# Expert one-hots, routing shares, block comparisons and head squares: other engines and other places in the queues

## The reference, cut to what matters

```
def L1_attn(x):                       # 16 heads of 16, blocks of 32 keys
    q, k, v = rope(x @ Wq.T), rope(x @ Wk.T), x @ Wv.T
    gate = q . mean of k over each block           # 8 blocks
    gate = -1e30 for later blocks, +1e30 for the own block
    sel = the 4 blocks with the highest gate
    p = softmax(q k^T / 4 where sel and causal)
    o = p @ v
    o = o * rsqrt(mean(o * o) + 1e-6) * o_norm_w   # for each head
    return o @ Wo.T

def L1_ffn(x):                        # F = 896, 8 experts of rank 32, top 2
    rw, sel = top_k(softmax(x @ Wg.T), 2); rw = rw / rw.sum()
    for k in range(2):
        mask = one_hot(sel[:, k])
        x1 = x @ W1.T + low_rank(A1, B1, mask)     # x3 the same way
        x2 = silu(x1) * x3
        out += (x2 @ W2.T + low_rank(A2, B2, mask)) * rw[:, k]
```

## Time and profile before

| | before |
|---|---|
| median of 3 runs | 714.51 us (713.04 to 714.55) |
| the profiled execution | 714.51 us, span 712.7 us |
| PE, DVE, ACT, POOL busy | 680.5, 491.6, 409.7, 284.7 us |
| chain that ended last | PE 77%, DVE 13%, ACT 5% |
| mean granted TensorE clock | 0.993 |

### The profile page before, as it was taken

One profiled execution on the slowest core, in us unless ns is written; L12 is line 12 of the kernel. 1 busy time (PEld: TensorE's weight loads), 2 busy tenths in 40 slices (PEclk: granted clock), 3 DMA queues, 4 the chain that ended last, 5 costly groups with the idle time before them and its releaser, 6 DMA issues.

```text
span 712.7 us, 13698 instructions
## 1 busy us (share of the span) xinstructions
PE 680.5 (95%) x4708; PEld 580.4 (81%) x4708; DVE 491.6 (69%) x1422; ACT 409.7 (57%) x1069; POOL 284.7 (40%) x289
## 2 busy tenths in 40 slices
PE   4999999999999999998999998999989999999997
PEld 3677888888889888887785655666889999999997
DVE  5898877877878787777695786767565454644544
ACT  2756158788797888888212578888753312222221
POOL 0573245556465554541004218999333320400000
PEclk9999999999999999999899999999999999999999
DMA  8902034453435354351900000200300000000000
GB/s 312 350 0 93 5 111 135 150 161 125 164 118 169 116 163 129 97 166 44 402 20 1 1 0 3 104 2 2 119 1 1 2 2 16 1 16 1 2 16 15
DMA packets 26725, 59.42 MB, mean 83 GB/s; under 512 B 3147, under 2 KB 12749, under 8 KB 26273
## 3 DMA queue, kind: packets, MB, share of 16 engines
q1 hardware_dynamic: 23584, 50.35, 20.7%
q0 software_dynamic: 3072, 8.20, 3.4%
HBM read 48.24 MB, written 10.49 MB: 82 GB/s over the span
## 4 chain that ended last, share of the span: by engine, by line
PE 77%; DVE 13%; ACT 5%; issue 3%; DMA 1%; POOL 0%; SPq 0%; DVEq 0%; ACTq 0%
PE bank L2164 11%; PE bank L1944 7%; PE bank L1878 6%; PE bank L2187 5%; PE bank L1935 5%; PE bank L2213 5%; PE bank L1964 4%; PE bank L1885 3%; PE bank L1955 3%; PE bank L2075 3%; PE bank L2006 3%; PE bank L2227 2%; PE bank L2133 2%; PE bank L2099 2%; ACT sb L1135 2%
## 5 line engine op out<-in xcount | busy, mean ns | idle before, releaser
L1031 ACT ACTIVATE sb<-bank,sb 128x256 f32<-128x256 f32 x128 | 59.6, 471 | 40.6 <-DVE sb L1497 33.1
L1497 DVE TENSOR_REDUCE sb<-bank 128x2 f32<-128x512 f32 x64 | 43.7, 683 | 47.5 <-PE bank L1944 47.1
L1944 PE MATMUL bank<-sb 128*128 128x256 f32 x256 | 66.1, 381 | 0.0
L1200 ACT ACTIVATE h_parts<-sb 128x256 fp32r<-128x256 f32 x56 | 23.4, 418 | 71.3 <-DVE sb L1733 43.4
L1724 DVE TENSOR_TENSOR sb<-sb,bank 128x256 f32<-128x256 f32 x56 | 23.5, 419 | 59.0 <-ACT sb L1164 59.0
L2164 PE MATMUL bank<-rounded,b_hi 128*128 128x256 f32 x224 | 63.6, 284 | 0.0
L2164 PE MATMUL bank<-rounded,b_lo 128*128 128x256 f32 x224 | 63.4, 283 | 0.0
L2164 PE MATMUL bank<-am_lo,b_hi 128*128 128x256 f32 x224 | 63.4, 283 | 0.0
L1164 ACT ACTIVATE sb<-bank 128x256 f32<-128x256 f32 x56 | 21.5, 383 | 63.4 <-PE bank L2164 63.3
L1038 ACT ACTIVATE sb<-sb 128x256 f32<-128x256 f32 x128 | 57.7, 504 | 0.1
L815 POOL DMA_INDIRECT expert_out<-sb x32 | 33.1, 1034 | 60.1 <-DVE sb L1439 44.2
(11 more groups left out here) (302 smaller groups left out, 1936.6 us busy)
## 6 DMA issues: line engine op xcount, KB each, us to landing
sb<-in_w_gate_up SPq DMA_DIRECT2D x32, 368.0 KB
sb<-in_w_down SPq DMA_DIRECT2D x32, 256.0 KB
sb<-in_w_pair SPq DMA_DIRECT2D x8, 704.0 KB
expert_out<-sb SPq DMA_DIRECT2D x1, 4096.0 KB, 22.5
sb<-expert_out SPq DMA_DIRECT2D x8, 512.0 KB, 7.3
sb<-in_w SPq DMA_DIRECT2D x1, 1792.0 KB, 13.8
sb<-in_b SPq DMA_DIRECT2D x1, 1792.0 KB, 7.0
sb<-in_sw_up SPq DMA_DIRECT2D x1, 1536.0 KB, 9.9
```

Of the source, the lines that this page charges most:

```text
L1031: act.activation(probs[:, u % 4, q, :], bank[3 + u % 2][:, q * S:(q + 1) * S], ACT.Exp, scale=-1.0, bias=row_min[:, u % 4, q:q + 1], accum ...
L1497: dve.tensor_reduce(row_min[:, u % 4, :], bank[3 + u % 2][:, :].rearrange("p (q n) -> p q n", q=QT), AX.X, ALU.min).then_inc(at_min, 1)
L1944: mm = pe.matmul(bank[3 + u % 2][:, q * S:(q + 1) * S], qb[i][:, h, b * S + q * P:b * S + (q + 1) * P], keys[:, h, b * S:(b + 1) * S], sta ...
```

## The change

- `expert_of` is made by DVE alone, in 16 instructions of 128x256 with the chosen expert as a per-partition scalar. The two small `one_of` and the two spreads on ACT go.
- The shares are transposed in two groups of eight, at j = 1 and j = 2, into banks 2 and 7, and DVE copies them out in its steps j = 1 and 2. The four `share_out` on ACT go. TensorE waits for the last copy at j = 3 and not at j = 5.
- All seven comparisons for the other sequences lie in DVE's loop steps: d = 1, 2, 3 at j = 0, d = 4, 5 at j = 1, d = 6, 7 at j = 2.
- The squares are one instruction at the end of s = 1, both sums and the epsilon come in s = 2, the root in s = 3 between `hidden_high(3, 0)` and `activated(1, 1)`, and the reciprocal at the end of DVE's s = 3.

```
 # POOL
-            pool.wait_ge(r1_step, 10 + 2 * NT)
+            pool.wait_ge(r1_step, 8 + 2 * NT)
 # ACT
-                if n == 3:
-                    for k in range(2):
-                        act.wait_ge(r1_step, 8 + 2 * NT + k)
-                        act.activation(expert_of[k].rearrange("p t (e r) -> p (t e) r", r=R1),
-                                       along(one_of[k].rearrange("p t e -> p (t e)"), (2, R1)), ACT.Copy).then_inc(r1_own, 1)
...
-            def share_out(n):
-                act.wait_ge(fill_mm, len(fills()) + n + 1)
-                act.activation(shareT[:, n // 2, n % 2 * CH:(n % 2 + 1) * CH], bank[SHARE_BANK[n]][:, :], ACT.Copy)\
-                    .then_inc(fill_out, 1)
...
-                if 0 < j < 5:
-                    share_out(j - 1)
...
+                if s == 3:
+                    act.wait_ge(on_step, 3)
+                    act.activation(o_sd, o_var, ACT.Sqrt).then_inc(on_act, 1)
...
-                if s in (1, 2):
-                    half = slice((s - 1) * HALF * H1, s * HALF * H1)
+                if s == 1:
                     act.wait_ge(bl_o, QUADS)
-                    act.activation(squares[:, half, :], o_tok.rearrange("p t (h d) -> p (t h) d", d=D1)[:, half, :], ACT.Square)\
-                        .then_inc(on_act, 1)
-                if s == 3:
-                    act.wait_ge(on_step, 3)
-                    act.activation(o_sd, o_var, ACT.Sqrt).then_inc(on_act, 1)
+                    act.activation(squares, o_tok.rearrange("p t (h d) -> p (t h) d", d=D1), ACT.Square).then_inc(on_act, 1)
 # DVE
             for k in range(2):
-                dve.tensor_tensor(one_of[k], along(table("iota")[:, 0:E1], (1, NT)), along(chosen1[:, :, k], (2, E1)),
-                                  ALU.is_equal).then_inc(r1_step, 1)
+                for i in range(NT):
+                    dve.tensor_scalar(expert_of[k][:, i, :].rearrange("p (e r) -> p e r", r=R1),
+                                      along(table("iota")[:, 0:E1], (2, R1)), chosen1[:, i, k:k + 1], None,
+                                      ALU.is_equal).then_inc(r1_own, 1)
...
-            for d in (1, 2, 3, 4):
-                compare(dve, rest_heads, beats_rest, rest_beats, d)
...
+            def shares_out(k, c):
+                dve.wait_ge(fill_mm, len(fills()) + 2 * k + c + 1)
+                dve.tensor_copy(shareT[:, k, c * CH:(c + 1) * CH], bank[2 + 5 * c][:, :]).then_inc(blk_step, 1)
...
+                if j < 3:
+                    for d in ((1, 2, 3), (4, 5), (6, 7))[j]:
+                        compare(dve, rest_heads, beats_rest, rest_beats, d)
                 if j in (1, 2):
-                    for d in ((5,), (6, 7))[j - 1]:
-                        compare(dve, rest_heads, beats_rest, rest_beats, d)
+                    for c in range(TOK // CH):
+                        shares_out(j - 1, c)
...
-                if s == 4:
-                    dve.wait_ge(on_act, 3)
-                    dve.reciprocal(o_inv, o_sd).then_inc(on_step, 1)
...
-                if s in (2, 3):
-                    half = slice((s - 2) * HALF * H1, (s - 1) * HALF * H1)
-                    dve.wait_ge(on_act, s - 1)
-                    dve.tensor_reduce(o_var_f[:, half], squares[:, half, :], AX.X, ALU.add).then_inc(on_step, 1)
-                if s == 3:
+                if s == 2:
+                    dve.wait_ge(on_act, 1)
+                    for half in (slice(0, HALF * H1), slice(HALF * H1, NT * H1)):
+                        dve.tensor_reduce(o_var_f[:, half], squares[:, half, :], AX.X, ALU.add).then_inc(on_step, 1)
                     dve.wait_ge(on_step, 2)
                     dve.tensor_scalar(o_var, o_var, 1.0 / D1, 1e-6, ALU.mult, ALU.add).then_inc(on_step, 1)
+                if s == 3:
+                    dve.wait_ge(on_act, 2)
+                    dve.reciprocal(o_inv, o_sd).then_inc(on_step, 1)
 # TensorE
-                    pe.wait_ge(r1_own, j + 1)
+                    pe.wait_ge(r1_own, NT * j + 4 * c + 4)
...
-            def shares(n):
-                pe.wait_ge(r1_share, 4 * n + 4)
-                pe.wait_ge(fill_out, len(fills()) + (n if n > 1 else 0))
-                for i in range(4):
-                    mm = pe.transpose(bank[SHARE_BANK[n]][:, i * P:(i + 1) * P], share_rep[:, 4 * n + i, :], ident)
-                mm.then_inc(fill_mm, 1)
+            def shares(k):
+                pe.wait_ge(r1_share, NT * (k + 1))
+                at_least(pe, blk_step, 3 + 2 * k if k else 0)
+                for c in range(TOK // CH):
+                    for i in range(4):
+                        mm = pe.transpose(bank[2 + 5 * c][:, i * P:(i + 1) * P], share_rep[:, NT * k + 4 * c + i, :], ident)
+                    mm.then_inc(fill_mm, 1)
...
                 if j == 1:
+                    pe.wait_ge(fill_out, len(fills()))
                     shares(0)
-                    shares(1)
-                if j in (3, 4):
-                    shares(j - 1)
-                if j == 5:
-                    pe.wait_ge(fill_out, len(fills()) + 4)
+                if j == 3:
+                    pe.wait_ge(blk_step, 7)
...
+                if j == 2:
+                    shares(1)
```

More of the change, by code:

```diff
@@ L73 @@
 VW = D1 + 1
-SCORE_BANK, SHARE_BANK = (3, 4, 0, 1), (2, 7, 7, 7)
+SCORE_BANK = (3, 4, 0, 1)
 F1, E1, R1 = 896, 8, 32
@@ L494, in program @@
         expert_of = [r2.take_b(NT, ER) for _ in range(2)]
-        one_of = [bias_g[:, k].rearrange("p q n -> p (q n)")[:, 0:NT * E1].rearrange("p (t e) -> p t e", e=E1) for k in range(2)]
         share_rep = Strip(region2, phase + 3 * NT * D, 2 * NT * P).take(2 * NT, P)
@@ L1726, in gated @@
                 if m == 0:
-                    dve.wait_ge(fill_out, len(fills()) + 4)
+                    dve.wait_ge(blk_step, 7)
                 if k == 0:
```

## The result

The changed kernel takes 721.8 us (median of 6 runs, 719.69 to 723.97) against 714.01 us (713.04 to 714.55) for the kernel before in the same job: a ratio of 1.011, 95% interval 1.0086 to 1.0135, or 7.8 us slower. Forecast were 718.0 us and a range up to 720.6. The profiled execution of the changed kernel took 723.6 us with a span of 721.8, 9.1 us more than the span before, and a mean granted clock of 0.983 against 0.993.

The account below looks back on a forecast made before the run. TensorE was taken to set the pace nearly everywhere, with loop delays reaching the feed-forward in full. From 714.51 us, 1.9 (loop start) + 0.6 (squares) + 1.0 (sums, root, reciprocal) = +3.5 gave 718.0 us; range 715.6 to 720.6.

Parts of the forecast that it names:

- a second fall of the clock: Rival: TensorE's waits at the turns of n = 2 and 3 lower its clock; 1.5 us more, 719.5 us; chance 0.12.
- The free start of the loop: Rival: ACT and TensorE do not wait for the minima, loop start costs +0.2; about 715.6 us; chance 0.12.
- the stall that goes: Rival: feed-forward table loads end early enough that TensorE never stops; -2.27 and -1.5 for the clock, 712.6 us; chance 0.10.
- the +0.6 of the squares: Feed-forward: one 1.8 us squares instruction on ACT delays the Silu of (2, 0), so `hidden1(3)` starts 0.6 us later.
- The one-hots: Ahead of the loop: 16 DVE instructions of 0.27 us each take 4.3 us; removing the ACT spreading gives nothing.
- the slow rate: Rival: one-hots on DVE take 6.2 us, ranks end 1.85 us later; 719.9 us; chance 0.14.
- The collision with POOL's share copies: Ahead of the loop: DVE's gate sum L1680 waits for POOL's second copy; part costs 0.9 us, without it zero.
- the late ranks: Ahead of the loop: ranks end at 423.2 in place of 419.15, so `own_bias(0)` starts 0.9 us later.
- The comparisons and the share copies: First loop steps: DVE's added work delays the turns; with the 0.9 us ahead of it, the loop starts 1.9 us later.
- two signs of being wrong: First Silu behind the loads starts before TensorE reaches `hidden1(4)`, or `values1(1)` does not move.
- Sums, root and reciprocal: Feed-forward: a 3.3 us stall ahead of `hidden1(4)` replaces 2.27 us ahead of `hidden1(5)`, clock fall on either side; +1.0 us.

Follow-up runs that it names:

- only_norm: Kernel before with only squares in one piece and sums, root and reciprocal moved as in the change; 715.15 us, ratio 1.0028.
- only_shares: Kernel before with only the share part: eight transposes at j = 1 and at j = 2, copies on DVE; 711.4 us, ratio 0.9972.
- only_one_hots: Kernel before with only the one-hots changed: 16 instructions on DVE, no spreading on ACT; 717.53 us, ratio 1.0052.
- only_compare: Kernel before with only the seven comparisons spread over j = 0, 1, 2; 716.99 us, ratio 1.0046.
- after_shares_as_before: Changed kernel with share copies back on ACT and share transposes at j = 1, 3, 4; 718.55 us, ratio 1.0065 to the kernel before.
- after: The changed kernel with all four parts, against the kernel before; 721.8 us, ratio 1.0110.
- after_rows_as_before: Changed kernel with the one-hots as before: two small ones on DVE, spread on ACT; 720.91 us, ratio 1.0083 to the kernel before.
- after_norm_as_before: Changed kernel with squares, sums, root and reciprocal back where they were; 720.15 us, ratio 1.0085 to the kernel before.
- turns_filled: Changed kernel with 9 and 11 extra transposes on TensorE ahead of the turns of n = 2 and 3, second share half used twice; 717.4 us, ratio 1.0049.

## Why the prediction was wrong

**The direction was right and the size was not.** One term failed. The prediction saw the two waits of TensorE at the turns of n = 2 and 3, sized them at 1.2 and 1.5 us (1.16 and 1.33 in the trace), and gave the clock behind them nothing in the forecast and 1.5 us in the rival "a second fall of the clock". It argued that the granted clock stayed at 1.00 around the waits that the loop already had. In fact the clock stood at 0.50 for 17.1 us, and that cost 6.5 us in the profiled execution (7.91 against 1.42 with the waits filled). By the medians it cost 4.4 us. The profiled execution was one of the longer ones, and the others left no trace, so how long the clock was down in the loop in them is not known. The forecast's +3.5 and this term make +7.9 us, against the +7.8 measured. The rival named the right mechanism, at a third to a quarter of its size.

With the waits filled the kernel is 3.5 us slower than before, which is the forecast's number. That it meets it so closely is in part luck: in that trace the loop cost 1.4 us where 1.9 was predicted, and the feed-forward 1.9 where 1.6 was.

Two of the rivals were added up wrongly. The free start of the loop and the stall that goes both leave out the +0.6 of the squares, which they give no reason to drop; with it they stand at 716.3 and 713.2 us.

**The one-hots.** Predicted 4.3 us, measured 4.24; the slow rate is out. The collision with POOL's share copies is there: 2.00 us for 1.23. The Trainium skill ("SBUF — State Buffer", Who interferes with whom) says that a DVE instruction with two inputs in SBUF contends with a GpSimd one that reads SBUF, and the trace agrees. It is this row that bears the rule out. The long L1328, which the prediction took for it, is by its row a TENSOR_SCALAR with one tensor to read, and so no case of two SBUF tensors. The bias came 0.70 us later, predicted 0.9. What the late ranks cost the loop is less: with the one-hots as before it starts only 0.35 us sooner.

**The comparisons and the share copies.** The working holds to a tenth up to where the clock falls. On the scale of before, the turn of n = 2 came at 428.68 us (predicted 428.7) and that of n = 3 at 430.53 (predicted 430.6). With the waits filled, `values1(0)` came at 433.86 and `values1(1)` at 438.72 (predicted 433.9 and 438.8). In the changed kernel itself they came at 435.16 and 443.99, so the sign of being right that the prediction named, `values1(1)` near 439, failed; neither of its two signs of being wrong came. With the waits filled the start of the loop cost 1.42 us up to `values1(13)`, predicted 1.9.

**The squares.** Predicted 1.8 us for the instruction, measured 1.90; +0.6 predicted for `hidden1(3)`, +0.61 measured, and +0.59 when the norm is changed alone.

**Sums, root and reciprocal.** A stall ahead of `hidden1(4)` with none ahead of `hidden1(5)`, as predicted; 2.94 us by the row where 3.3 by the slots (some 3.1 by the row) were expected. The net of the move was +1.34 us with a fall of the clock on either side, and 192.68 - 191.92 = +0.76 with none on either side (only_norm against only_shares), predicted +1.0. The prediction priced the fall at 1.5 us on both sides, so that it cancelled; it cost 1.5 us after and 0.9 before, which is the other 0.6. So the rival in which the stall goes and nothing takes its place is out.

**The sum of the parts.** By their ratios the four parts alone make +3.7 (one-hots), +3.3 (comparisons), -2.0 (shares) and +2.0 us (norm), 7.0 in all, and the whole 7.8. The agreement hides how they act. In two of them the fall of the clock is already included (10.2 us in only_one_hots, 6.8 in only_compare); together the parts give one long fall, and the shares turn from a gain to a loss: without them the change would be 3.2 us less slow (1.0110 against 1.0065).

**What stays open.** Which waits bring the clock down, and what keeps it down. A wait of 1.26 us stood in the loop of before and of only_norm with the clock at 1.00; one of 1.17 us was followed by a fall in after_shares_as_before and in only_compare. In the 4 us ahead of the wait the matmuls were already sparser there (PE is busy 3.13 and 3.47 us of them, against 3.86 in the kernel before and 3.85 in only_norm), but no run varies this by itself. In the three traces with both waits the clock fell inside the second, 0.4 to 0.9 us after it had begun, so the second did not start the fall by its full length; no run fills only one of the two. Nor is it shown why the fall behind the stall in the feed-forward comes in some executions only.

## What to carry to other kernels

A new wait on an engine whose clock is granted by its work isn't priced by its own length. Where a change thins out TensorE's matmuls or sets a second wait of about 1 us behind a first, look at the granted clock there, and set into the range the whole stretch that could run at half clock: here 2.5 us of waits brought up to 6.5 us more. Work that was woven into a gap should stay there: the moved comparisons left ACT waiting 1.63 us for DVE, and the displaced ones in only_one_hots put the first minimum behind them at 424.46 us. And a change of several parts is worth taking apart: one of the four was a gain by itself.

## What the runs showed of the hardware

- With two waits of 1.16 and 1.33 us, 1.85 us apart in their ends, TensorE's clock was at 1.2 GHz for 17.1 us (after, after_rows_as_before, after_norm_as_before), in a loop in which PE was then busy all the time by its rows (in after 2.00 of 2 us in each window from 430 us on). With one wait of 1.17 us it was there for 6.8 us, with one of 2.6 us for 6.8 or 10.2 us. The Trainium skill ("TensorE: Matmul & The Clock Gate", A second HAM failure mode: psum-queue depth-cycling) tells of a bf16 kernel whose short idle times between groups of matmuls make the clock go back and forth between its two levels. The traces here agree that short waits go with a fall, but show one long fall in place of many.
- One and the same fall of 3.4 us cost 0.9 us in one place of the feed-forward and 1.5 us in another.
- Transposes whose result nobody reads kept the clock at 1.00 through the same places (turns_filled) and the kernel was 4.4 us faster.
- The time of one and the same kernel moves in steps with the mean granted clock: 723.6 us at 0.983 in the profiled execution of the change and 720.8 at 0.986 or 719.7 at 0.988 in others. Differences below about 1 us between two profiles say nothing as long as the falls of the clock in both aren't compared.
